# VectorE's seven compares of a pair of groups: four in the odd step and three in the even one, with the flags loaded behind the compares

## The reference

```python
h = jnp.maximum(_layernorm(x, axis=-1), 0.0)
h = h @ W + b                                   # layer 0
msgs = edge_w[:, None] * h[edge_src]
agg = jax.ops.segment_sum(msgs, edge_dst, num_segments=N_NODES)
deg = jax.ops.segment_sum(edge_w, edge_dst, num_segments=N_NODES)
x = x + jax.nn.relu(agg / (deg[:, None] + 1e-06))

h = jnp.maximum(_layernorm(x, axis=-1), 0.0)
msg_in = jnp.concatenate([h[src], edge_features], axis=-1)      # layer 1
messages = jax.nn.gelu(msg_in @ W_msg + b_msg)
agg = jax.ops.segment_sum(messages, tgt, num_segments=h.shape[0])
x = x + jax.nn.gelu(((1.0 + eps) * h + agg) @ W_upd + b_upd)
```

## Time and profile before

| | |
|---|---|
| median of 3 runs | 3355.64 us (3353.7 to 3358.54) |
| the profiled execution, its own time | 3358.17 us |
| its span, first to last instruction | 3356.3 us |
| TensorE matmul / weight load busy | 92% / 89% |
| VectorE, ScalarE, POOL busy | 77%, 58%, 72% |
| compares L1016 | 1372, 1604 ns each, 2119.5 us |
| gathers L455 | 1274 in layer 0 and 1276 in layer 1, about 945 ns each |

### The profile page before, as it was taken

One profiled execution on the slowest core, in us unless ns is written; L12 is line 12 of the kernel. 1 busy time (PEld: TensorE's weight loads), 2 busy tenths in 40 slices (PEclk: granted clock), 3 DMA queues, 4 the chain that ended last, 5 costly groups with the idle time before them and its releaser, 6 DMA issues.

```text
span 3356.3 us, 102112 instructions
## 1 busy us (share of the span) xinstructions
PE 3086.3 (92%) x37939; PEld 3001.4 (89%) x37940; DVE 2578.4 (77%) x3125; ACT 1947.4 (58%) x6683; POOL 2424.6 (72%) x2565
## 2 busy tenths in 40 slices
PE   3999999888898889888889999999999999999998
PEld 3999898888888888888889999999999999999998
DVE  8777777777777777777677777777777777777776
ACT  5666666656666656666555555555555555555554
POOL 5777777777777777777377777777777777777774
PEclk9999999999999999999999999999999999999999
DMA  6232332332222332222233333333333333333332
GB/s 138 68 75 67 71 72 67 70 72 68 67 67 67 70 72 69 67 67 68 54 90 99 98 98 98 96 96 95 97 96 97 96 97 95 98 96 97 98 97 67
DMA packets 497289, 280.12 MB, mean 83 GB/s; under 512 B 255166, under 2 KB 430782, under 8 KB 497258
## 3 DMA queue, kind: packets, MB, share of 16 engines
q1 hardware_dynamic: 415658, 195.99, 21.3%
q0 software_dynamic: 81600, 83.72, 12.3%
HBM read 274.00 MB, written 5.50 MB: 83 GB/s over the span
## 4 chain that ended last, share of the span: by engine, by line
PE 43%; POOL 27%; issue 14%; DVE 11%; DVEq 3%; POOLq 0%; DMA 0%; ACT 0%; ACTq 0%
POOL rows L455 27%; PE ps L686 21%; PE ps L693 10%; DVE pick_all L1016 10%; PE ps L714 5%; PE ps L831 5%; PE ps L820 1%; DVEq L1058 1%; DVEq L1054 1%; DVE sums_sb L1066 0%; PE ps L778 0%; PE ps L742 0%; DVEq L1207 0%; DVEq L1067 0%; DMA rows<-h_table,idx 0%
## 5 line engine op out<-in xcount | busy, mean ns | idle before, releaser
L1016 DVE TENSOR_SCALAR pick_all<-src_bc,node_f 128x2688 bf16<-128x2688 int16 x1372 | 2119.5, 1604 | 106.0 <-issue 103.9
L686 PE MATMUL ps<-parts,pick_all 128*128 128x192 bf16 x19159 | 1651.0, 246 | 190.3 <-DVE pick_all L1016 182.1
L686 PEld LDWEIGHTS ps<-parts,pick_all 128*128 128x128 bf16 x19159 | 1578.0, 98 | 234.9 <-issue 149.5
L455 POOL DMA_INDIRECT rows<-p_table,idx x1276 | 1204.0, 944 | 450.7 <-issue 348.7
L455 POOL DMA_INDIRECT rows<-h_table,idx x1274 | 1204.5, 945 | 398.6 <-issue 389.0
L693 PE MATMUL ps<-parts,pick_all 128*128 128x192 bf16 x9555 | 853.7, 246 | 1.8
L693 PEld LDWEIGHTS ps<-parts,pick_all 128*128 128x128 bf16 x9555 | 793.8, 98 | 7.6 <-issue 5.3
L543 ACT ACTIVATE h_sb<-iota,dw 128x72 f32<-128x72 f32 x1568 | 405.8, 342 | 0.0
L543 ACT ACTIVATE onehot<-iota,dw 128x72 f32<-128x72 f32 x1568 | 405.8, 342 | 0.0
L1180 DVE TENSOR_TENSOR room<-ps,rows 128x512 f32<-128x512 f32 x196 | 135.5, 691 | 270.2 <-PE ps L831 266.6
L1066 DVE TENSOR_TENSOR sums_sb<-sums_sb,ps 65x72 f32 (+1 forms) x392 | 88.3, 225 | 331.1 <-PE ps L714 311.7
(11 more groups left out here) (103 smaller groups left out, 1368.4 us busy)
## 6 DMA issues: line engine op xcount, KB each, us to landing
src_bc<-last_src SPq DMA_DIRECT2D x196, 448.0 KB
ea<-in_edge_attr_dram SPq DMA_DIRECT2D x196, 256.0 KB
src_bc<-last_src SPq DMA_DIRECT2D x196, 224.0 KB
rows<-p_table,idx POOLq DMA_INDIRECT x1276
rows<-h_table,idx POOLq DMA_INDIRECT x1274
x_sb<-in_x_dram SPq DMA_DIRECT2D x6, 224.0 KB, 4.4
h_table<-h_sb SPq DMA_DIRECT2D x6, 224.0 KB
p_table<-h_sb SPq DMA_DIRECT2D x6, 224.0 KB
```

What stands on the lines that cost most here:

```text
L455: nc.gpsimd.indirect_dma_start(out=rows[:, s, j, 0:D], out_offset=None, in_=table[:, :], in_offset=bass.IndirectOffsetOnAxis(ap=idx[:, s, ...
L686: last = nc.tensor.matmul(psG[(s + shift) % 2], pick[layer][(s + shift) // 2 % 2][:, n, at:at + P], parts[:, n, :], start=(n == 0), stop=( ...
L1016: last = nc.vector.tensor_scalar(pick[layer][i][:, c * KB:(c + 1) * KB, :], src_bc[:, i, :, 0:w], node_f[:, c:c + 1], None, ALU.is_equal)
```

## The change

Half 0 of a pair's one-hot gets units 0 to 3 (four compares) and half 1 units 4 to 6 (three): the odd step makes four and the even step three. This holds in both layers, in the second pick ahead of each loop too; the count of compares stays. And at the head of a body the flags are loaded behind the compares of step 0, no longer ahead of them.

```diff
+    FIRST = UNITS // 2 + 1
...
             def pick_half(layer, i, half):
                 w = width(layer, i)
-                for c in range(half * UNITS // 2, (half + 1) * UNITS // 2):
+                for c in range(0, FIRST) if half == 0 else range(FIRST, UNITS):
...
             def first(b, last_body):
-                more = more_flags(b)
                 for s in range(SLOTS):
                     if not last_body or s == 0:
                         next_pick(0, b, s)
+                    if s == 0:
+                        more = more_flags(b)
                     if s % 2 == 0:
                         even = base_of(b, s)
...
             def second(b, last_body):
-                more = more_flags(b)
                 for s in range(SLOTS):
                     if not last_body or s == 0:
                         next_pick(1, b, s)
+                    if s == 0:
+                        more = more_flags(b)
                     if s % 2 == 0:
                         even = base_of(b, s)
```

## The result

The changed kernel takes 3315.04 us in the median (3314.02 to 3317.03), the kernel before 3355.88: 40.8 us less, a ratio of 0.9876 with a 95% interval of 0.986 to 0.9892. The forecast was 3300 us in a range of 3294 to 3318. The direction and the range held, and so did the mechanism of the gain in layer 1. 15 us of the 56 that I promised are missing, and 12.2 of them have one place: the stage behind the last tick.

The account below looks back on a forecast made before the run. Layer 0 was taken as bound by POOL, layer 1 by the other engines, with TensorE waiting for compares. 44.9 us (earlier last gather) plus 12.1 behind it, less 1 for handoffs, gave 56: 3355.64 to 3300 us, range 3294 to 3318.

Parts of the forecast that it names:

- TensorE's waits are the bound of layer 1, and both go: Layer 1: TensorE's waits of 1.33 and 0.22 us for VectorE's compares vanish, a body drops from 33.75 to 32.20 us.
- the flags cost 0.6 us: Pair A, the body's first: loading the flags ahead of the compares delays them about 0.6 us; moving it is free.
- Layer 0 gives nothing: Layer 0: POOL's gather issues bound it at 32.46 us a body without a hole, so the change gains nothing there.
- POOL is late next: Layer 1: POOL's 32.46 us a body becomes the bound; its last gather starts at 3273.5 instead of 3318.40, 44.9 us.
- Behind the last gather, 2.46 + 3.90 us: Layer 1's end: last gather to its use 2.46 us, last message sum to last tick 3.90; 6.36 replaces 18.44, saving 12.1.
- The step that failed: Layer 1's end: the last tick no longer lags the last gather by 18.44 us, since the other engines wait for the landing.
- the raw sum of 57.0: Whole kernel: 44.9 us from the earlier last gather plus 12.1 us behind it.
- 1 us taken off: Between the last landing and the message sum: 1 us subtracted from 57.0 for handoffs, leaving 56.
- The odd step's cover of 1.18 us: Odd step, VectorE: 2.71 us idle before the message sum absorbs the extra 1.53 us compare, leaving 1.18; costed at nothing.
- The rival that made the kernel slower by an exposed compare: Layer 1, between a pair's message sums: the extra compare is exposed, 1.51 us a body, 72 us, 3428 us; 3%.
- The rule on GpSimd's port: Odd step: two-port compares lock GpSimd out, so a gather lands up to 1.53 us later; about 3301 instead of 3300.

Follow-up runs that it names:

- before_light: The kernel before with one indirect gather fewer in each group (22 a body instead of 26, part of each sum left out): 3314.92 us, ratio 0.9881.
- after_light_b: The changed kernel with one indirect gather fewer in each group (22 a body instead of 26, part of each sum left out): 3114.06 us, ratio 0.928.
- compares_only_b: The changed kernel with the flags loaded ahead of the compares again, so only the split 4/3 stays: 3315.93 us, ratio 0.9884.
- warm_c: The changed kernel plus TensorE filler matmuls (30, 48 and 88) in the last body of each layer: 3301.31 us, ratio 0.9839.
- flags_only_b: The changed kernel with the split 3/4 of before, so only the flags are moved: 3322.89 us, ratio 0.9903.
- after: The changed kernel itself, with both parts of the change: 3315.04 us, ratio 0.9876.
- six_one_light: The changed kernel with 22 gathers a body, and six compares in the odd step and one in the even: 3112.57 us, ratio 0.9269.
- The two further splits: The changed kernel with 22 gathers a body and odd/even compares split five/two (3116.06 us) or six/one (3112.57 us).
- warm: The changed kernel plus TensorE filler matmuls in the last body of each layer, on a chip with TensorE pauses: 5588.72 us, ratio 0.9917.
- warm_b: The changed kernel plus the same last-body TensorE filler matmuls, run again on another chip with TensorE pauses: 5474.87 us, ratio 0.9892.

## Why the prediction was right, and where it fell short

**TensorE's waits are the bound of layer 1, and both go.** Right. I had 32.20 us a body for TensorE alone and 33.1 for the flags alone; the runs show 32.32 and 33.08. That the flags cost 0.6 us was right (0.67). They are not needed: the split alone reaches 32.32.

**Layer 0 gives nothing.** Right in the full kernel (last gather at 1626.62 for 1627.35), and before_light and after_light_b show why: without POOL's 32.46 the change takes a body from 31.08 to 28.33.

**POOL is late next.** Right, by less than I wrote: the others need 32.32 and not 32.20, and their bodies take POOL's pace only in the last third of the layer. For the sum that makes no difference, since POOL issues without a wait from the first gather on. I put the last gather at 3273.5; it started at 3275.35, 1.85 us later. The first gather of the layer came 2.16 us later, at 1683.69 for the 1681.53 that I said would not move, and the step was 0.0002 us shorter, 0.3 us over 1275. That first gather lies at 1679.55 in compares_only_b, 1681.53 before, 1682.66 in warm_c, 1683.69 in the changed kernel and 1684.41 in flags_only_b. The granted clock from 1630 to 1650, by stretches of 10 us, was 1.00 and 1.00, 1.00 and 1.00, 0.70 and 0.96, 0.60 and 0.89, 0.67 and 0.50. The later ones have the lower clock; no run separates that from other causes.

**Behind the last gather, 2.46 + 3.90 us.** Near: 3281.93 - 3275.35 = 6.58, for the 6.36 of the sum. Part of this is luck, since the last window products ran at the low clock. In warm_c, where they did not, it is 5.55.

**The step that failed** is an unspoken one: "Behind it, the last tick came 18.44 us later because the others lagged; now they are waiting for the landing". I took the gain out of that and kept the 19.5 us behind the tick as they were. But the wait that makes the last gather the bound is idle time of TensorE, and its clock in the stage behind fell with it. The term for the update stage should have been 31.7. Against the raw sum of 57.0: 57.0 - 1.85 - 0.2 - 12.2 = 42.7, the difference of the two spans. The forecast of 56 had 1 us taken off that did not occur, and the profiled executions were 2.3 us above their median before and 0.4 after, which makes 1.9. So the missing 15 us are 14.2 - 1 + 1.9. warm_c, in which TensorE doesn't idle, lands at 3301.31 for the 3300 forecast.

**The odd step's cover of 1.18 us** was on the safe side. The trace of after shows 1.62 left, and six_one_light shows that even the idle time ahead of the message sum is not its end: the next consumer was 3.9 us away. The rival that made the kernel slower by an exposed compare was weaker than I wrote, and no split tried reached the point from which it decides. The two further splits were tried in the kernel with 22 gathers only.

**The rule on GpSimd's port.** The trace of after has a direct look at it. In the changed kernel:

```profile
3243.73 6.16 DVE L1018 TENSOR_SCALAR pick_all<-src_bc,node_f 128x2688 bf16<-128x2688 int16 x4
...
3249.13 0.95 POOL L457 DMA_INDIRECT rows<-p_table,idx  x1 [0.30 <-issue]
...
3251.74 0.69 DVE L1183 TENSOR_TENSOR room<-ps,rows 128x512 f32<-128x512 f32 x1 [1.58 <-DMA rows<-p_table,idx]
...
3253.27 4.65 DVE L1018 TENSOR_SCALAR pick_all<-src_bc,node_f 128x2688 bf16<-128x2688 int16 x3
...
3256.62 0.94 POOL L457 DMA_INDIRECT rows<-p_table,idx  x1 [0.30 <-issue]
...
3259.17 0.69 DVE L1183 TENSOR_TENSOR room<-ps,rows 128x512 f32<-128x512 f32 x1 [0.71 <-DMA rows<-p_table,idx]
```

The gathers at 3249.13 and 3256.62 are the last of their groups; they start under running compares, which end 0.76 and 1.30 us later, and are used 2.61 and 2.55 us after their start. The last one of all, at 3275.35 with VectorE idle, is used 2.52 us after it. So the compares delay a landing by 0.09 us at most in these rows, and neither the 0.76 nor the 1.30 us shows in their landings. The Trainium skill ("SBUF — State Buffer", Who interferes with whom) has GpSimd locked out for the whole of a two-port instruction; these compares behave as if they were not in such a mode, and no run here tells the mode itself.

## What to carry to other kernels

Read a loop's period from one row that comes back in each turn, and set it against each engine's own need; the next bound, here POOL's 26 issues of 1.2484 us, is then known before the edit. Where a change turns a busy engine into one that waits, estimate the stage behind the wait anew: TensorE's idle time ahead of a TensorE-paced tail cost 12 us here, and some hundred filler matmuls gave them back. The cover of a moved instruction ends at the first consumer that would wait, not at the idle time in front of the next instruction on its engine.

## What I had not expected

The granted clock fell with TensorE still busy for 5.23 and 5.89 us of two stretches of 10, and was at 0.50 through the 30 us behind, although TensorE was busy for 9.4 and 10.0 of 10 us in the first two stretches of it. The same stage ran at 1.0 in the kernel before, after stretches with 9.19 and 7.93 us busy. The Trainium skill ("TensorE: Matmul & The Clock Gate", Part 1) ties the clock to the array's activity. The fall behind idle time, from 1.00 over 0.85 and 0.67 to 0.50, agrees with it. That the clock stayed low under busy update products is a thing that these rows show and I did not foresee; why it did is open.

On two chips TensorE took its instructions with pauses of 0.4 to 1.1 us in this kernel's variants, and the kernel before took two thirds longer there (5639 us for 3356). Later, on another chip, the program of warm and warm_b ran at 3301 us. What made the pauses is open.
